# Cross attention: the exponentials of the first four heads as one instruction, their maxima subtracted on POOL and their sums taken on DVE

## What is computed

```
qh = (x @ wq.T + bq).reshape(Bx, N, H, d).transpose(0, 2, 1, 3)
kh = (memory @ wk.T + bk).reshape(Bx, -1, H, d).transpose(0, 2, 1, 3)
vh = (memory @ wv.T + bv).reshape(Bx, -1, H, d).transpose(0, 2, 1, 3)
a = jax.nn.softmax(jnp.einsum('bhnd,bhmd->bhnm', qh, kh) / jnp.sqrt(jnp.float32(d)), axis=-1)
ca = jnp.einsum('bhnm,bhmd->bhnd', a, vh).transpose(0, 2, 1, 3).reshape(Bx, N, Cx)
```

## Time and profile before

| | |
|---|---|
| median of 3 runs | 868.1 us (867.17 to 868.54) |
| the profiled execution | 866.22 us |
| its span, first to last instruction | 864.4 us |
| busy: PE, DVE, ACT, POOL | 719.8, 572.0, 490.6, 373.3 us |
| granted TensorE clock, mean | 0.904 of full speed |

### The profile page before, as it was taken

The page is one execution under the profiler, slowest core; times in us unless marked ns, Lnnn a source line. Parts: engine busy times, 40 slices in busy tenths (PEclk is TensorE's granted clock), DMA queues, the critical chain, the costliest instruction groups (busy, mean ns, idle before and its releaser), DMA issues.

```text
span 864.4 us, 15642 instructions
## 1 busy us (share of the span) xinstructions
PE 719.8 (83%) x5368; PEld 467.4 (54%) x5368; DVE 572.0 (66%) x2196; ACT 490.6 (57%) x1121; POOL 373.3 (43%) x416
## 2 busy tenths in 40 slices
PE   5758798797878976788979899779897998879997
PEld 4436464564665745654546565545564664565443
DVE  5776877768755657648776967757776455763623
ACT  4336384563736535455676595695775855554542
POOL 4465645456533445343354554465443234532100
PEclk9888999879886977899989899999899898799999
DMA  8610010100100000101130221210302001004253
GB/s 260 204 43 2 14 43 14 28 17 13 45 13 2 2 0 1 61 24 59 38 80 23 55 65 32 64 30 13 80 26 62 13 26 30 14 19 131 65 136 89
DMA packets 37162, 41.83 MB, mean 48 GB/s; under 512 B 14346, under 2 KB 23772, under 8 KB 36956
## 3 DMA queue, kind: packets, MB, share of 16 engines
q1 hardware_dynamic: 37083, 40.83, 17.3%
HBM read 28.75 MB, written 2.62 MB: 36 GB/s over the span
## 4 chain that ended last, share of the span: by engine, by line
PE 47%; DVE 29%; ACT 11%; POOL 8%; issue 3%; DMA 1%; SPq 0%; DVEq 0%; POOLq 0%; ACTq 0%
PE act_psum L623 5%; PE moe_psum L633 5%; DVE work L1145 4%; PE dve_psum L455 4%; ACT work L877 4%; PE act_psum L722 3%; POOL work L1537 3%; PE dve_psum L526 3%; PE act_psum L516 3%; DVE res_nrm L1125 2%; PE dve_psum L725 2%; PE act_psum L785 2%; DVE work L1168 2%; DVE stats L1115 2%; DVE sumsq L1175 2%
## 5 line engine op out<-in xcount | busy, mean ns | idle before, releaser
L1537 POOL TENSOR_TENSOR work<-work,rinv 128x512 f32<-128x512 f32 (+1 forms) x80 | 87.6, 1110 | 106.6 <-DVE rinv L1135 105.4
L1519 POOL TENSOR_SCALAR rstd<-mv 128x2 f32<-128x2 f32 x72 | 16.8, 234 | 139.0 <-DVE mv L1118 139.0
L1578 POOL TENSOR_TENSOR hT<-hT,work 128x512 f32<-128x512 f32 x32 | 40.7, 1272 | 71.3 <-DVE work L1168 71.3
L455 PE MATMUL dve_psum<-wqkv,hTs 128*128 128x512 f32 x128 | 67.4, 653 | 2.0 <-ACT hTs L1024 2.0
L877 ACT ACTIVATE work<-work,nbias,rnorm 128x128 f32<-128x128 f32 x128 | 61.1, 478 | 0.0
L855 ACT COPY v_loc<-act_psum 77x512 f32<-77x512 f32 (+2 forms) x72 | 41.3, 582 | 34.4 <-PE act_psum L460 16.5
L442 PE MATMUL act_psum<-ident,res_nrm 128*128 128x128 f32 x96 | 26.6, 366 | 37.0 <-DVE res_nrm L1125 37.0
L1520 POOL TENSOR_TENSOR rstd<-rstd,neg_half 128x2 f32<-128x2 f32 x72 | 52.3, 726 | 6.0
L855 ACT COPY hT<-act_psum 128x512 f32<-128x512 f32 (+1 forms) x60 | 31.2, 523 | 39.4 <-PE act_psum L516 21.8
L1164 DVE TENSOR_TENSOR hT<-dve_psum,tab_a 128x512 f32<-128x512 f32 x32 | 22.1, 689 | 44.1 <-PE act_psum L467 26.8
L1584 POOL TENSOR_TENSOR v_loc<-v_loc,rnorm 128x512 f32<-128x512 f32 x32 | 33.3, 1062 | 38.8 <-DVE rnorm L1187 38.8
(11 more groups left out here) (227 smaller groups left out, 2077.7 us busy)
## 6 DMA issues: line engine op xcount, KB each, us to landing
ahead<-cwT_dram SPq DMA_DIRECT2D x128, 64.0 KB, 2.0
v_loc<-v_loc SPq DMA_DIRECT2D x24, 256.0 KB, 3.7
kT<-cwT_dram SPq DMA_DIRECT2D x80, 64.0 KB, 2.1
qT<-cwT_dram SPq DMA_DIRECT2D x48, 64.0 KB, 2.1
wqkv<-in_wqkv_dram SPq DMA_DIRECT2D x2, 768.0 KB
res_nrm<-in_x_dram SPq DMA_DIRECT2D x4, 256.0 KB, 3.1
w_m<-in_w_m_dram SPq DMA_DIRECT2D x1, 1024.0 KB, 8.5
v_loc<-v_loc SPq DMA_DIRECT2D x8, 128.0 KB, 3.1
```

Of the source, the lines that this page charges most:

```text
L455: nc.tensor.matmul(bank[:], h, attn_w[:, k * INNER:(k + 1) * INNER], start=True, stop=True)\
L1537: nc.gpsimd.tensor_tensor(some, some, by.unsqueeze(2).to_broadcast(list(some.shape)), ALU.mult).then_inc(ready[u], 1)
L1578: nc.gpsimd.tensor_tensor(own, own, partners[u][:, t % 2, k, :], ALU.add).then_inc(turned_ready[u], 1)
```

## The change

In the cross attention the first four heads of each tile (`WHOLE` = 0) are handled as in the local attention. DVE leaves out the nbias of that half. POOL subtracts the four maxima from the half's 4 x 154 scores (`less_maxima`) and signals `less_max`. ACT takes one exponential over 616 columns with scale 1/4, without bias and accumulated sum. DVE sums the four heads (`tensor_reduce` over the half) before the first reciprocal. The second half stays as it is. On POOL the subtraction for tile 0 is in the step that was empty, and that for tile t+1 stands ahead of the divisions of tile t.

```diff
-                def exponentials_by_halves(u, number, b, weights, scale_of, whole=()):
+                def exponentials_by_halves(u, number, b, weights, scale_of, whole_scale=1.0):
                     for g in range(2):
-                        if g in whole:
+                        if g == WHOLE:
                             act.wait_ge(less_max[u], number - sm_local(0, 0) + 1)
                             some = weights[:, HALF * g:HALF * g + HALF, :]
-                            nc.scalar.activation(some, some, ACT.Exp).then_inc(exp_done[u], 1)
+                            nc.scalar.activation(some, some, ACT.Exp, scale=whole_scale).then_inc(exp_done[u], 1)
                             continue
-                        act.wait_ge(peak_ready[u], peaks_done(number, g))
+                        act.wait_ge(peak_ready[u], number + 1)
...
-                        exponentials_by_halves(u, sm_cross(t), t % 2, cprob[u][t % 2], lambda i: CA_DH ** -0.5)
+                        exponentials_by_halves(u, sm_cross(t), t % 2, cprob[u][t % 2], lambda i: CA_DH ** -0.5, CA_DH ** -0.5)
...
-                    invert_sums(u, number, b)
+                    invert_sums(u, number, b, cprob[u][b])
...
                                 last.then_inc(dve_emptied, 1)
+                            if g == WHOLE:
+                                continue
                             dve.wait_ge(dve_emptied, dve_item["s_ca", t, u, 2 * g + 1] + 1)
...
                 def cross_attention_steps(u):
-                    yield
-                    for t in range(TILES):
+                    def less_maxima(t, u):
+                        pool.wait_ge(dve_emptied, dve_item["s_ca", t, u, 2 * WHOLE + 1] + 1)
+                        some = cprob[u][t % 2][:, HALF * WHOLE:HALF * WHOLE + HALF, :]
+                        top = peak[u][:, t % 2, HALF * WHOLE:HALF * WHOLE + HALF]
+                        nc.gpsimd.tensor_tensor(some, some, top.unsqueeze(2).to_broadcast([P, HALF, CTX]), ALU.subtract)\
+                          .then_inc(less_max[u], 1)
+
+                    less_maxima(0, u)
+                    yield
+                    for t in range(TILES):
+                        if t + 1 < TILES:
+                            less_maxima(t + 1, u)
                         divide_half(u, sm_cross(t), t % 2, cprob[u][t % 2], 0, probs_lo_ready)
                         divide_half(u, sm_cross(t), t % 2, cprob[u][t % 2], 1, probs_hi_ready)
                         yield
```

More of the change, by code:

```diff
@@ L131, in is_deferred @@
     return u < DEFER
-def peaks_done(number, g):
-    lead = sm_cross(0)
-    return number + 1 if number < lead else lead + 2 * (number - lead) + g + 1
 def half_done(number, g):
@@ L907, in scale_of @@
                             return rnorm[u][:, t, h:h + 1]
-                        exponentials_by_halves(u, sm_local(l, t), t % 2, lprob[u][:, t % 2], scale_of, whole=(WHOLE,))
+                        exponentials_by_halves(u, sm_local(l, t), t % 2, lprob[u][:, t % 2], scale_of)
                     def take_pt_hi(t, u):
```

## The result

The changed kernel takes 883.64 us (median of 4 runs, 882.36 to 884.06), the kernel before beside it on the same chip 867.63 us (4 runs). The ratio is 1.0173, with a 95% interval of 1.0155 to 1.0190: slower by 15 us by the ratio and 16 by the medians. The forecast was 873.2 us, 5.1 us slower, with a range that ended at 878.5. The sign was right, the size three times too small.

A forecast was written before the change was run, and what follows sets the result against it. No engine was full; the chain passed through every engine, with the path from DVE's last maximum to the exponentials' end deciding. Stretches 1.8 + 1.65 + 0.2 + 1.5 = +5.15 us on 868.1 gave 873.2 us, range 866.5 to 878.5.

The forecast's parts named there:

- Durations: Per tile: ACT's exponential over 616 columns 720 ns, DVE's sum 787 ns, POOL's subtraction 1.22 us.
- What ACT saves POOL takes back: about +0.1: Per tile, from DVE's last first-half maximum to the end of all eight exponentials: 3.57 us before, 3.63 after.
- A, +1.8: Cross-attention stretch from 262 to 300 us: +1.8 us, mostly DVE's sum twice on the chain at +0.83.
- C, +0.2: Cross-attention stretch from 662 to 707 us: PE has deferred experts between, so only 0.1 + 0.1 = +0.2 us.
- B, +1.65: Cross-attention stretch from 326 to 363 us: +1.65 us, with +1.1 at the first division and +0.6 at tile 1's.
- The division of tile 1 ends at about 345.5, and PE gets to its projection 0.6 later: In the stretch from 326 to 363 us: POOL's division of tile 1 delays PE's projection, +0.6 us.
- D, +1.5: Cross-attention stretch from 738 to 776 us: +1.5 us, from delayed divisions and DVE's sum, less nbias excess.
- fits into the 0.87 us in which DVE waits for PE: Tile 2, stretch from 326 to 363 us: DVE's sum hidden in idle time at 340.19; tile's net -0.2 us.
- The clock: A shift outside the four stretches through the clock granted to PE after longer idling; named, not in the sum.
- The fourth case, blocking (878.8): POOL's added work blocks DVE, both norm applies doubling in stretches B and D: 878.8 us, chance 0.1.
- Hidden: Rival: what one stream is late the other covers across the stretches, so no change, 868.2 us; chance 0.2.
- faster: Rival: subtraction starts at once, nbias excess is gained and DVE's sum fits into idle time: 865.0 us; chance 0.15.

The follow-up runs named there:

- the subtraction in the path: Changed kernel without DVE's sum and without the merged exponential: POOL subtracts, ACT takes four exponentials with accumulated sums; 878.42 us, ratio 1.0123.
- the one beside it: Kernel before plus a 128x616 POOL subtraction on unused data at the changed kernel's places, ScalarE not waiting for it; 877.75 us, ratio 1.0109.
- the second profile of before: Kernel before, unchanged, run and profiled once more; 868.35 us, ratio 1.0002.
- the narrow run: Kernel before plus a POOL subtraction on unused data at the changed kernel's places and with its waits, only 128x4 wide; 869.90 us, ratio 1.0026.

## Why the prediction was wrong in its size

- *Durations.* Right within 1%, all three, from neighbouring forms and a slope.
- *"What ACT saves POOL takes back: about +0.1."* Right. In the changed kernel the subtraction that starts at 347.78 and the exponentials behind it end at 351.3, 3.5 us where I had 3.63; the subtraction in the path and the one beside it cost about the same (shift 10.7 and 10.3 us); and ACT waits for POOL in 14 of 16 tiles.
- *A, +1.8.* +1.65 measured, and with the sum alone +1.66: the two sums of 0.83 us on the chain, as worked out. *C, +0.2:* +0.70.
- *B, +1.65.* +4.70. The first division was nearly right: PE's wait for it grew by 1.52 us (5.86 against 4.34), where I had +1.1. The step that failed is "The division of tile 1 ends at about 345.5, and PE gets to its projection 0.6 later": the projection came 2.2 us later (353.67 against 345.45 in the first profile, 8.2 us late, where tile 0's transposes had been 6.0 late). Two things make that up. The division ended at 351.33, or 346.6 without the 4.7 us by which PE was late when B began, 1.1 us behind my 345.5, and PE waited 2.47 us for its first half. And PE's four groups of transposes behind that wait ran at the lower clock, so that they were 9.1 us late at the first and 10.4 at the fourth. Then PE waited 1.98 us at 359.10 for the division of tile 2, for which I had counted nothing. I had put the subtraction of the next tile at the moment at which its scores were ready in the trace of before, but these scores come later themselves once PE has waited for the division before and DVE has taken its sum. The added instruction on unused data shows the same step without the path: 10.3 us ahead of the divisions, 4.8 behind them.
- *D, +1.5.* +3.38, the same step: PE waits 2.44 us for the first division (2.15 before), then 2.56 at 770.92 and 1.19 at 780.4, where it had no such wait before.
- *DVE's sum.* My terms for it are about 3.5 of the 5.15 us: 1.66 in A, 0.63 in B, 1.2 in D. Alone it cost 9.4: 1.66 in A, but 2.42 in B and 2.5 in D with what follows, and 2.8 outside. What failed is that it "fits into the 0.87 us in which DVE waits for PE". Alone it was covered there only in part: DVE's idle time at that place was still 0.51 us (0.86 in the second profile of before). And it had held back the first division, for which PE waited 5.17 us instead of 4.35, a term that I had not for the sum:

```profile
339.95 1.14 PE L581 MATMUL dve_psum<-ident,work 128*77 128x128 f32 x4 [5.17 <-POOL work L1537]
...
345.01 0.32 DVE L1145 CUSTOM_DVE_ANT_0 work<-dve_psum,no_mask 128x154 f32<-128x154 f32 x1 [0.51 <-PE dve_psum L570]
```

- *The clock.* I named the shift through the granted clock and left it out of the sum. In B 3.1 us could be had back by a better one. Outside the stretches 4.7 us are left, 1.15 of them the start; for the other 3.6 the traces show more time at the lower level (from 366 to 430 us 3.4 us before and 13.6 after), but no run removed it, so they are not shown to be the clock's.
- *The fourth case, blocking (878.8).* Its first cause is real: the norm apply and the second half's nbias are blocked beside POOL's work (3.00 us at 348.93 against 1.10; the second half's nbias lasts 437 ns in the mean, where it had 198 before, so the excess that I counted as gone moved from the first half's to the second's, where ACT doesn't wait for it). I cited the Trainium skill there, page "SBUF — State Buffer", section "Who interferes with whom"; the rows agree, also where the partner was a division (2.08 us in the narrow run). But in B one of the two norm applies is blocked (3.00 us) and the other isn't (1.10 us at 334.98), and in D it is the same (2.99 and 1.10), where I had put both. And the added instruction costs 4.8 us behind the divisions, with a norm apply of 2.04 us, against 10.3 ahead of them, with one of 2.92. So blocking is a part whose size isn't shown; the larger step is POOL's own queue, which I had priced too low.
- *Hidden and faster* are excluded by both halves of the change: each alone is slower by over 1%.

The range ended at 878.5, since I gave the clock no term and the queue too small ones, and let the fourth case reach it only by half. The two halves alone lie at 878.1 and 878.4, inside; both together lie outside.

## What to carry to other kernels

Before an instruction is put ahead of others in an in-order queue, take the three separately: how long it waits there, how long it runs, and who waits for what stands behind it. Here a late start alone cost 2.9 us, the full instruction behind the ready work 4.8, and the same one ahead of it 10.3; an instruction on unused data at the same place tells such a price without touching the path. Slack that is read in the old trace belongs to the old timing; where two streams and PE take turns, a delay of one uses up the slack of the next, and the sum of local excesses came to a third of the loss here. When runs are compared by their traces, take the difference of the start out first: here it was as large as some of the effects. And the cheapest gain was in taking a step out of the path (a scaling folded into the copy that precedes it), not in moving it to an engine with room.

## What the runs showed of the hardware that I had not expected

- Four transposes in a row take 0.60 us at the full grant and 1.06 to 1.14 at the lower level. In B of the second profile of before the clock is at the lower level from 332.0 to 342.2 and from 349.0 to 355.8 us, in the changed kernel from 333.1 to 346.8, 350.2 to 353.6 and 360.5 to 363.9. So work that is moved by a few us can fall into such a time or out of it. Whether that is why half the width of the added POOL instruction cost 8.4 of the 10.3 us is not shown.
- The start differs from run to run. In the changed kernel's profile DVE's norm apply fell beside POOL's table products and took 2.55 us; in the first profile of before it was through ahead of them, 1.11 us at 11.71. The rows of the changed kernel:

```profile
12.63 2.55 DVE L1119 TENSOR_SCALAR res_nrm<-res_nrm,mv,rstd 128x128 f32<-128x128 f32 x4
12.74 0.89 POOL L1560 TENSOR_TENSOR tab_a<-kT 128x256 f32<-128x256 f32 x1
```

- An exponential over 616 columns with a bias per row took 808 ns, without one 717; 91 ns for the bias operand. The Trainium skill, page "ScalarE: Activation LUTs", section "What ACT_TABLE_LOAD costs", gives about 93 ns for each pointer operand and 186 ns + 0.833 ns a column without one. An estimate from that is 699 ns for 616 columns: the rows agree within 3%. I had taken the price from the slope of ACT's copies instead.
